# A recurrent memory layer and a gated feed-forward block: the normalised input split as rows and turned by transposing DMAs in place of TensorE

## The reference

```
xn = LN(x)
# recurrent memory, over the 2048 steps
q, k, v = xn Wq', xn Wk', xn Wv'
r_t = q_t M' ;  M <- 0.99 M + v_t' k_t / 4          (M is 128 x 128, starts at M0)
s = (r Wo') * sigmoid(gate)
# feed-forward
h = LN(xn) * gamma + beta
y = silu(h dequant(q1) + b1)                          (512 -> 2048)
z = y dequant(q2) + b2                                (2048 -> 512)
out = x + s * silu(xn + 0.5 z)
```

## Time and profile before

| | |
|---|---|
| median of 3 runs | 1291.49 us (1291.27 to 1292.08) |
| the profiled execution | 1291.07 us, span 1289.2 us |
| busy | PE 93%, DVE 88%, ACT 70%, POOL 62% |
| granted TensorE clock, mean | 0.986 |
| a chunk in the middle | 74.94 us |

### The profile page before, as it was taken

One profiled execution on the slowest core, in us unless ns is written; L12 is line 12 of the kernel. 1 busy time (PEld: TensorE's weight loads), 2 busy tenths in 40 slices (PEclk: granted clock), 3 DMA queues, 4 the chain that ended last, 5 costly groups with the idle time before them and its releaser, 6 DMA issues.

```text
span 1289.2 us, 18645 instructions
## 1 busy us (share of the span) xinstructions
PE 1204.1 (93%) x5900; PEld 608.0 (47%) x5900; DVE 1132.0 (88%) x1962; ACT 906.9 (70%) x1558; POOL 805.4 (62%) x766
## 2 busy tenths in 40 slices
...
DMA packets 41620, 65.68 MB, mean 51 GB/s; under 512 B 11696, under 2 KB 11952, under 8 KB 41008
## 3 DMA queue, kind: packets, MB, share of 16 engines
...
## 4 chain that ended last, share of the span: by engine, by line
PE 77%; DVE 11%; issue 5%; ACT 3%; POOL 3%; DMA 1%; SPq 0%; DVEq 0%; POOLq 0%; ACTq 0%
PE blk L466 28%; PE blk L484 27%; PE side L427 10%; DVE blk L722 5%; PE side L451 4%; DVE y_split L713 2%; PE side L443 2%; DVE y_split L708 1%; PE side L410 1%; DVE g_lo L692 1%; PE side L444 1%; PE side L445 1%; PE side L436 1%; POOL g_rows L1004 1%; ACT blk L603 1%
## 5 line engine op out<-in xcount | busy, mean ns | idle before, releaser
L722 DVE TENSOR_TENSOR blk<-blk,ratio_rows 128x512 f32<-128x512 f32 x960 | 644.9, 690 | 88.9 <-PE blk L484 85.3
L603 ACT ACTIVATE blk<-blk,ratio 128x512 f32<-128x512 f32 x768 | 508.1, 666 | 228.5 <-PE blk L466 218.6
L466 PE MATMUL blk<-h_split,q_sb 128*128 128x512 f16 x2048 | 613.8, 382 | 10.2 <-issue 4.9
L484 PE MATMUL blk<-w_sb,y_split 128*128 128x512 f16 x2048 | 610.6, 380 | 6.5 <-DVE blk L722 4.3
L484 PEld LDWEIGHTS blk<-w_sb,y_split 128*128 128x128 f16 x2048 | 199.4, 98 | 253.5 <-DVE blk L722 14.1
L466 PEld LDWEIGHTS blk<-h_split,q_sb 128*128 128x128 f16 x2048 | 196.3, 98 | 223.9 <-issue 36.3
L610 ACT ACTIVATE y_full<-blk,par,last 128x512 f32<-128x512 f32 x256 | 201.3, 786 | 112.4 <-PE blk L466 112.3
L713 DVE SCALAR_TENSOR_TENSOR y_split<-y_full,up,y_split 128x512 f16<-128x512 f32 x256 | 218.8, 855 | 0.0
L1016 POOL CAST h_split<-h_full 128x512 f16<-128x512 f32 x64 | 52.9, 826 | 251.5 <-ACT h_full L565 251.5
L708 DVE TENSOR_SCALAR y_split<-y_full,up 128x512 f16<-128x512 f32 x256 | 159.4, 623 | 5.0 <-ACT y_full L610 5.0
L1004 POOL TENSOR_SCALAR g_rows<-xt,mv,gs 128x512 f32<-128x512 f32 x64 | 141.5, 2218 | 0.1
...
## 6 DMA issues: line engine op xcount, KB each, us to landing
...
x_again<-in_x SPq DMA_DIRECT2D x256, 64.0 KB, 1.9
out<-z_rows SPq DMA_DIRECT2D x256, 64.0 KB, 1.7
w_sb<-in_q SPq DMA_DIRECT2D x4, 1024.0 KB, 13.8
ratio_rows<-ratio_dram SPq DMA_DIRECT2D x4, 1024.0 KB, 7.6
y_split<-in_q SPq DMA_DIRECT2D x1, 1024.0 KB, 10.5
h_split<-in_q SPq DMA_DIRECT2D x1, 1024.0 KB, 12.7
z_rows<-in_q SPq DMA_DIRECT2D x1, 1024.0 KB, 14.6
```

The lines of the kernel that those rows point to most:

```text
L466: mm = pe.matmul(blk[J % 2][:], q1_sb[:, g, j // 4, w, j % 4 * P:(j % 4 + 1) * P], a[:, c % 2, g, :], start=(g == 0 and n == 0), stop=(g = ...
L484: mm = pe.matmul(blk2[:, i, :], y[:, J % Y_RING, rows], w2_sb[:, j, part, :], start=(j == 0 and n == 0), stop=(j == FB - 1 and n == len(te ...
L603: act.activation(blk[J % 2][:], blk[J % 2][:], ACT.Copy, scale=ratio1[:, at:at + 1]).then_inc(blk_scaled, 1)
L722: dve.tensor_tensor(blk2[:, i, :], blk2[:, i, :], ratio2_rows[:, j, :], ALU.mult).then_inc(blk2_scaled, 1)
```

## The change

- `normalise` becomes a product and a sum: x * gs + g_shift, and writes over xt (g_rows is now a name for xt). `rows` gets two more small operations for g_shift.
- From the second chunk on the split is made of rows: ACT casts a tile of g_rows to float16 (`g_high`, steps 33, 35, 37, 39), POOL takes the difference (`g_low`, steps 34, 36, 38, 40). Both lie in g_split.
- SP then issues for each tile two transposing DMAs (`turn_g`), g_split to g_hi and to g_lo: 8 in a chunk. The first waits until the last qkv product of the current chunk is done (step 37). The turns of TensorE and their banks are gone.
- h_full is made in SBUF by two operations: ACT gamma * g_hi + beta (`h_part`, steps 48, 50, 52, 54), which waits for all eight transposes, and DVE h_full + gamma * g_lo (`h_sum`, steps 49, 51, 53, 55). The POOL halves follow at steps 50, 52, 54, 56 (before: 54, 57, 59, 62).
- normalise stands at POOL's steps 31, 33, 35, 37 (before: 36, 38, 40, 42). load_x of the next chunk waits for `g_low` in place of `normalise`, and stands behind the transposes.
- The first chunk is turned by TensorE as before.

```diff
--- before.py
+++ after.py
@@ -18,7 +18,7 @@
 ZERO_POINT = 128.0
 G_SCALE = 1024.0
 TOP = 2.0 ** 14
-ROW_STEPS = 10
+ROW_STEPS = 12
...
 TILE_AT, JOB_AT = (1, 13, 25, 37), (0, 4, 7, 10, 13)
-TURN_AT = (51, 54, 56, 59)
-
-QKV_LAG, QKT_LAG, R_LAG, S_LAG, GHIGH_LAG, HFULL_LAG = 1, 1, 1, 1, 1, 2
+
+QKV_LAG, QKT_LAG, R_LAG, S_LAG = 1, 1, 1, 1
+
+G_HIGH_AT, G_LOW_AT = (33, 35, 37, 39), (34, 36, 38, 40)
+H_PART_AT, H_SUM_AT, H_SPLIT_AT = (48, 50, 52, 54), (49, 51, 53, 55), (50, 52, 54, 56)
 GATE_AT = (16, 17, 21, 29)
 
 STATS_AT, MOMENTS_AT = (0, 1, 2, 3), (5, 6)
 FIRST_STATS_AT, FIRST_MOMENTS_AT = (18, 20, 22, 24), (26, 27)
-MASK_LAG, MEM_LAG, GLOW_LAG, YHIGH_LAG, YLOW_LAG = 1, 1, 3, 1, 2
-
-HSPLIT_LAG = 3
-NORMALISE_AT = (36, 38, 40, 42)
+MASK_LAG, MEM_LAG, YHIGH_LAG, YLOW_LAG = 1, 1, 1, 2
+
+NORMALISE_AT = (31, 33, 35, 37)
...
-        g_rows = sb("g_rows", [P, NT, H], F32)
+
+        g_rows = xt
+        g_split = sb("g_split", [P, 2, NT, H], F16)
...
+            def turn_g(c):
+
+                sp.wait_ge(h_done, 4 * c)
+                sp.wait_ge(qkv_done, 4 * c)
+                for i in range(NT):
+                    sp.wait_ge(g_lo_rows, NT * (c - 1) + i + 1)
+                    for n, to in enumerate((g_hi, g_lo)):
+                        sp.dma_start_transpose(to[:, :, i * P:(i + 1) * P], g_split[:, n, i, :]).then_inc(g_turned, 16)
...
@@ -371,13 +383,15 @@
 
             for c in range(NCH + 1):
                 if 0 < c < NCH - 1:
-                    g_wait(sp, c)
+                    sp.wait_ge(g_lo_rows, NT * c)
                     load_x(c + 1)
                 for i in range(NT):
                     if c > 0:
                         store(c - 1, i)
                     if c < NCH:
                         load_again(c, i)
+                if c < NCH - 1:
+                    turn_g(c + 1)
...
-            def turn(c, k, bank):
-
-                if k == 0:
-                    g_wait(pe, c)
-                for i in range(NT):
-                    mm = pe.transpose(bank[:, i * P:(i + 1) * P], g_rows[:, i, k * P:(k + 1) * P], ident[:])
-                mm.then_inc(turn_done, 1)
...
-                if job == "turn":
-                    turn(c, i, bank)
-                elif job == "qkv":
-                    if i == 0:
-                        pe.wait_ge(g_lo_done, 4 * c + 4)
+                if job == "qkv":
+                    if i == 0 and c == 0:
+                        pe.wait_ge(g_lo_done, 4)
+                    elif i == 0:
+                        pe.wait_ge(g_turned, 2 * NT * 16 * c)
...
-            def g_high(c, k, bank):
-                act.wait_ge(turn_done, 4 * c + k + 1)
-                wait(act, qkv_done, 4 * c)
-                made = act.activation(g_hi[:, k, :], bank[:], ACT.Copy)
-                if c == 0:
-                    made.then_inc(first_g_hi_done, 1)
-
-            def h_whole(c, k, bank):
-                if c == 0:
-                    act.wait_ge(h_scales, 1)
-                    act.wait_ge(turn_done, k + 1)
-                wait(act, h_done, 4 * c + k - 1)
+            def first_g_high(k, bank):
+                act.wait_ge(turn_done, k + 1)
+                act.activation(g_hi[:, k, :], bank[:], ACT.Copy).then_inc(first_g_hi_done, 1)
+
+            def first_h(k, bank):
+                act.wait_ge(h_scales, 1)
+                act.wait_ge(turn_done, k + 1)
+                wait(act, h_done, k - 1)
                 act.activation(h_full[:, k % 2, :], bank[:], ACT.Identity,
                                bias=beta_s[:, k:k + 1], scale=gamma_s[:, k:k + 1]).then_inc(h_full_done, 1)
+
+            def g_high(c, i):
+                act.wait_ge(g_done, NT * c + i + 1)
+
+                wait(act, g_turned, 2 * NT * 16 * (c - 1))
+                act.activation(g_split[:, 0, i, :], g_rows[:, i, :], ACT.Copy).then_inc(g_hi_rows, 1)
+
+            def h_part(c, k):
+                act.wait_ge(g_turned, 2 * NT * 16 * c)
+                act.wait_ge(h_done, 4 * c + k - 1)
+                act.activation(h_full[:, k % 2, :], g_hi[:, k, :], ACT.Identity,
+                               bias=beta_s[:, k:k + 1], scale=gamma_s[:, k:k + 1]).then_inc(h_part_done, 1)
...
-                if at := job_behind(G, GHIGH_LAG, "turn"):
-                    g_high(*at, side[JOB_BANK[G - GHIGH_LAG]])
-                if at := job_behind(G, HFULL_LAG, "turn"):
-                    h_whole(*at, side[JOB_BANK[G - HFULL_LAG]])
+                if at := next_chunk(G, G_HIGH_AT):
+                    g_high(*at)
+                if at := next_chunk(G, H_PART_AT):
+                    h_part(*at)
...
-            def g_low(c, k, bank):
-
-                dve.wait_ge(h_full_done, 4 * c + k + 1)
-                if c == 0:
-                    dve.wait_ge(first_g_hi_done, k + 1)
+            def first_g_low(k, bank):
+
+                dve.wait_ge(h_full_done, k + 1)
+                dve.wait_ge(first_g_hi_done, k + 1)
                 dve.tensor_tensor(g_lo[:, k, :], bank[:], g_hi[:, k, :], ALU.subtract).then_inc(g_lo_done, 1)
+
+            def h_sum(c, k):
+                dve.wait_ge(h_part_done, 4 * (c - 1) + k + 1)
+                dve.scalar_tensor_tensor(h_full[:, k % 2, :], g_lo[:, k, :], gamma_s[:, k:k + 1], h_full[:, k % 2, :],
+                                         ALU.mult, ALU.add).then_inc(h_full_done, 1)
...
-                if at := job_behind(G, GLOW_LAG, "turn"):
-                    g_low(*at, side[JOB_BANK[G - GLOW_LAG]])
+                if at := next_chunk(G, H_SUM_AT):
+                    h_sum(*at)
...
                 step(pool.tensor_tensor(t[3], mean, rs[:, c % 3, :], ALU.mult))
-                pool.tensor_tensor(nmr[:, c % 3, :], t[3], row_const[:, MINUS_ONE, :], ALU.mult
+                step(pool.tensor_tensor(nmr[:, c % 3, :], t[3], row_const[:, MINUS_ONE, :], ALU.mult))
+                step(pool.tensor_tensor(t[3], mean, gs[:, parity, :], ALU.mult))
+                pool.tensor_tensor(g_shift[:, parity, :], t[3], row_const[:, MINUS_ONE, :], ALU.mult
                                    ).then_inc(rows_done, 1)
...
             def normalise(c, i):
                 if i == 0:
                     pool.wait_ge(rows_done, c + 1)
-                    wait(pool, turn_done, 4 * c)
-                pool.tensor_scalar(g_rows[:, i, :], xt[:, i, :], mv[:, c % 2, i, 0:1],
-                                   gs[:, c % 2, i:i + 1], ALU.subtract, ALU.mult).then_inc(g_done, 1)
+                pool.tensor_scalar(g_rows[:, i, :], xt[:, i, :], gs[:, c % 2, i:i + 1],
+                                   g_shift[:, c % 2, i:i + 1], ALU.mult, ALU.add).then_inc(g_done, 1)
+
+            def g_low(c, i):
+                pool.wait_ge(g_hi_rows, NT * (c - 1) + i + 1)
+                pool.tensor_tensor(g_split[:, 1, i, :], g_rows[:, i, :], g_split[:, 0, i, :], ALU.subtract
+                                   ).then_inc(g_lo_rows, 1)
...
-                if c < NCH - 1 and e in NORMALISE_AT:
-                    normalise(c + 1, NORMALISE_AT.index(e))
-                if at := job_behind(G, HSPLIT_LAG, "turn"):
+                if at := next_chunk(G, NORMALISE_AT):
+                    normalise(*at)
+                if at := next_chunk(G, G_LOW_AT):
+                    g_low(*at)
+                if at := next_chunk(G, H_SPLIT_AT):
                     h_high(*at)
                     h_low(*at)
```

More of the change, by code:

```diff
@@ L62 @@
         SIDE[TILE_AT[_i] + JOB_AT[_n]] = (_job, _i)
-    SIDE[TURN_AT[_i]] = ("turn", _i)
 def build(nc, x, wqkv, wo, gate, m0, q1, q2, b2, params, out):
@@ L84, in side_job @@
             return None
-        job, i = SIDE[e]
-        c += 1 if job == "turn" else 0
-        return (job, c, i) if c < NCH and not (job == "turn" and c == 0) else None
+        return (SIDE[e][0], c, SIDE[e][1]) if c < NCH else None
     def job_behind(G, lag, kind):
@@ L97, in finishing, with next_chunk @@
         return (c - 1, at.index(e)) if c > 0 and e in at else None
+    def next_chunk(G, at):
+        c, e = divmod(G, STEPS)
+        return (c + 1, at.index(e)) if c < NCH - 1 and e in at else None
     def fc1_step(G):
@@ L401, in bank_free @@
                     pe.wait_ge(s_out, n)
-                else:
-                    pe.wait_ge(g_lo_done, n)
-            def turn(c, k, bank):
-                if k == 0:
-                    g_wait(pe, c)
-                for i in range(NT):
-                    mm = pe.transpose(bank[:, i * P:(i + 1) * P], g_rows[:, i, k * P:(k + 1) * P], ident[:])
-                mm.then_inc(turn_done, 1)
             def run_side(G):
@@ L640, in _ @@
             for k in range(KC):
[L641 to L642 removed]
+                first_h(k, first_turn_bank[k])
+                first_g_high(k, first_turn_bank[k])
             act.wait_ge(q1_scale, 1)
@@ L866, in _ @@
             top_of_q1(2)
-            g_low(0, 0, first_turn_bank[0])
+            first_g_low(0, first_turn_bank[0])
             top_of_q1(3).then_inc(tops_made, 1)
```

(2 more changed lines are left out.)

14 lines of the change are left out of this document (6 added, 8 removed).

## The result

The changed kernel takes **1312.11 us** (median of 4 runs, 1311.58 to 1312.81) against 1291.38 for the kernel before, measured beside it: ratio 1.0166, interval 1.0153 to 1.0179. It is slower by 20.7 us; forecast were 10.5.

A forecast was written before the change was run, and what follows sets the result against it. DVE was taken to bound the kernel around chunk boundaries and PE the rest. Start -3.9, boundary +10.2 and middle +4.5 sum to +10.8 us on the profiled 1291.07, so 1302 us, range 1268 to 1322.

The forecast's parts named there:

- the likeliest case: At the chunk boundary, DVE-POOL collisions fill what DVE gained; C from 1.3 to 2.9, 1294 to 1318 us; chance 0.48.
- C: Time per chunk that DVE loses waiting for POOL around the boundary: 1.8 us, bounded by 0 and 4.2.
- Start, -3.9: Before the loop, POOL's four shorter normalisations let DVE's first g_lo come earlier: -3.9 us, once.
- Boundary, +0.68 a chunk: DVE's stretch up to the mask: -1.12 us from its changed list, plus collisions of 1.8; times 15, +10.2 us.
- Middle, +0.3 a chunk: Steps 34 to 40: g_low can meet L708 and L713; +0.3 us a chunk, from -0.4 to +1.0; times 15, +4.5.
- all four meet: Middle of the chunk, upper bound: all four g_low collide with DVE's L708 and L713, +1.0 us a chunk.
- The reading of rows 4: DVE operations with SBUF inputs, L708 and L713, wait for POOL's two-SBUF-input operation in flight, less 0.2 us.
- DVE alone sets the boundary: Around the boundary of two chunks DVE, 24.55 us without idle time, sets the time and PE follows.
- Transposes, no wait: Eight transposing DMAs take 9.1 us in all, inside 11.9 before h_part; holds up to 1.25 us each.
- POOL falls between: Rival: POOL's operations fall between DVE's, C 0 to 0.9, the middle costs nothing; 1272 us; chance 0.22.
- TensorE alone: Rival: TensorE sets the boundary too, DVE having unseen slack, so removed turns and the read wait are gained; 1252 us; chance 0.04.
- late transposes: Rival: eight transposes at 1.9 us each land 3.3 us late in each chunk; 1352 us or more; chance 0.13.

The follow-up runs named there:

- three steps' distance: Changed kernel with g_shift at step 29, g_high and g_low a step later, and h_part, h_sum and POOL halves three steps apart: 1290.19 us, ratio 0.9992.

## Why the prediction was right in kind and wrong in size

The direction was right, and so was the mechanism at the boundary; the time (1312) lies inside the range (1268 to 1322) and inside the likeliest case's own (1294 to 1318). The size was off by a factor of two: 20.7 us in place of 10.5. That 1312 still fell within the case's bounds is luck: they were laid out for C, the collisions at the boundary, and C was right, while the excess came from another term.

- *Start, -3.9*: right (-4.03 at the first qkv), and a further -1.06 over the whole first chunk.
- *Boundary, +0.68 a chunk*: right, +0.67. The collisions worked out (0.45, 0.36, 0.37, and 0.6 later) appeared as 0.47, 0.30, 0.39 and 0.6 (L724 took 1.09 at 668.49 against 0.47 alone).
- *Middle, +0.3 a chunk*: **this is the term that failed**, +1.10, over 15 chunks 16.5 us instead of 4.5. Four statements behind it were wrong. "In the rest of the chunk PE sets it" and "DVE has slack" don't hold from 682.17 to 695.86, where DVE works without a gap; the kernels with g_shift at step 29 got back 0.61 and 0.55 there. "Worth nothing in itself" was said of POOL's work, because its sum stayed the same; but 0.56 us of it moved ahead of L1056, and that operation had until then been nearly over when L708 came. "L1004 held up nobody" was read from the one L713: in the same trace the L708 at 631.81 takes 0.79 with 0.51 of a L1004 left. And "1.0 us that ACT's slack hides" was 1.30 and was hidden only in part. The upper bound of +1.0 that I had named ("all four meet") was for another mechanism and still too low.
- *The reading of rows 4*: L708 has one tensor in SBUF, y_full, and not two like L713; it waits all the same (1.52, and 1.20 and 1.21 in the later traces), so the forecast doesn't suffer.
- *DVE alone sets the boundary*: too strong. The kernel with doubled turns shows PE 0.48 us behind (1.76 less 1.28). It did no harm to the sum, since in the changed kernel DVE is the bound by far.
- *Transposes, no wait*: right in the steady chunks, by a margin of 0.3 us and not the 2.8 expected (11.9 less 9.1). Each took 1.30 us of SP and 2.5 to land, not 0.9 and 1.9, so that even the bound of 1.25 each was passed. ACT waited for them 6 times, 4.2 us in all in the trace, of which only a part reached PE.
- *The rivals*: "POOL falls between" didn't happen, though three steps' distance takes 0.75 off the chunk; "TensorE alone" forecast a faster kernel and is out, and so are "late transposes" (15 x 3.3 us), since half of them left out changed nothing.

The chunks add up: -4.03 to the first qkv, -1.06 in chunk 0, +25.8 in chunks 1 to 14 and -0.2 after them make +20.5, the difference of the two spans (1309.7 less 1289.2).
